# Edge sorting in two parts, with a fixed share of the gathers done during the second part

## The reference

```python
# x [6250,256], src,dst,edge_weight [100000]
x = x + gnn(layernorm(x), W, src, dst, edge_weight)
x = x + moe(layernorm(x))

def gnn(x, W, edge_row, edge_col, edge_val):      # edge_row=src, edge_col=dst
    h = einsum('nd,od->no', x, W)
    msgs = edge_val[:, None] * h[edge_col]
    return segment_sum(msgs, edge_row, num_segments=6250)

def moe(x):
    topk_vals, topk_idx = top_k(x @ gate_w + gate_b, 2)
    h = relu(einsum('bsh,ehf->bsef', x, w1) + b1)
    sel = take_along_axis(einsum('bsef,efh->bseh', h, w2) + b2, topk_idx)
    y = x + sum(softmax(topk_vals) * sel)
    return layernorm(y) * gamma + beta
```

## Time and profile before

| | |
|---|---|
| median of 3 runs | 2410.16 us (2407.57 to 2418.26) |
| profiled execution, first to last instruction (span) | 2018.8 us |
| median less span | 391.4 us |
| busy: PE, PEld | 1467.5 (73%), 1163.1 (58%) |
| busy: DVE, ACT, POOL | 965.3 (48%), 638.6 (32%), 1155.4 (57%) |
| mean granted TensorE clock | 0.850 |
| sort: to the first gather of the sums | 0 to 381.3 us |
| sums: first to last gather | 381.3 to 1436.1 us |

### The profile page before, as it was taken

One profiled execution on the slowest core, in us unless ns is written; L12 is line 12 of the kernel. 1 busy time (PEld: TensorE's weight loads), 2 busy tenths in 40 slices (PEclk: granted clock), 3 DMA queues, 4 the chain that ended last, 5 costly groups with the idle time before them and its releaser, 6 DMA issues. The chain is left out here.

```text
span 2018.8 us, 34171 instructions
## 1 busy us (share of the span) xinstructions
PE 1467.5 (73%) x7822; PEld 1163.1 (58%) x7823; DVE 965.3 (48%) x2285; ACT 638.6 (32%) x1737; POOL 1155.4 (57%) x1167
## 2 busy tenths in 40 slices
PE   7006889477777776777767777767369999999964
PEld 4005888344454554545545554545249999988853
DVE  8999999433323233233253233343653333333348
ACT  4624999000011110110110100101444544444465
POOL 1001444577777777777777777777615554544534
PEclk9558999677788888787778788878789999999987
DMA  5102000233333333333333333333652222243366
GB/s 178 37 19 75 7 6 6 67 104 104 104 104 104 103 104 104 104 104 104 104 99 103 103 103 104 104 104 104 146 183 70 70 90 86 91 147 125 107 197 219
DMA packets 107317, 201.66 MB, mean 100 GB/s; under 512 B 19988, under 2 KB 68747, under 8 KB 107144
## 3 DMA queue, kind: packets, MB, share of 16 engines
q0 software_dynamic: 52672, 139.93, 23.9%
q1 hardware_dynamic: 39720, 42.83, 6.4%
q10 hardware_dynamic: 14880, 18.35, 2.8%
HBM read 165.17 MB, written 35.86 MB: 100 GB/s over the span
## 5 line engine op out<-in xcount | busy, mean ns | idle before, releaser
L858 POOL DMA_INDIRECT hbuf<-xn_rows,ix x832 | 801.0, 963 | 267.9 <-issue 233.2
L950 PE MATMUL bank<-hbuf,picks 128*128 x2032 | 649.4, 461 | 288.3 <-SPq L846 287.7
L950 PEld LDWEIGHTS bank<-hbuf,picks 128*128 128x128 f32 x2032 | 417.4, 223 | 502.2 <-issue 448.6
L887 DVE TENSOR_SCALAR picks<-iota_two,marks 128x256 f32<-128x256 f32 x832 | 330.6, 441 | 677.2 <-PE bank L950 660.2
L1022 ACT ACTIVATE agg<-bank 128x256 f32<-128x256 f32 x49 | 18.8, 383 | 850.3 <-PE bank L950 850.3
L406 POOL DMA_INDIRECT edge_groups<-work,dest_i x56 | 80.7, 1441 | 279.9 <-DVE work L637 267.1
L766 PE MATMUL bank<-work 128*128 128x192 bf16 x1568 | 146.7, 251 | 115.2 <-DVE work L630 115.2
L1568 PEld LDWEIGHTS bank<-rowsT,w_sb 128*128 128x128 f32 x1744 | 212.3, 193 | 28.8 <-issue 24.1
L1568 PE MATMUL bank<-rowsT,w_sb 128*128 128x128 f32 x1744 | 215.7, 277 | 17.7 <-issue 17.7
L1504 POOL DMA_INDIRECT expert_out<-y_sb,to_i x112 | 111.1, 992 | 185.9 <-DVE y_sb L1613 183.0
L1578 PE MATMUL bank<-w_sb,hT 128*128 128x256 f32 x872 | 206.9, 380 | 0.0
(11 more groups left out here) (261 smaller groups left out, 1411.6 us busy)
## 6 DMA issues: line engine op xcount, KB each, us to landing
w_sb<-in_L_ffn_w_dram ACTq DMA_DIRECT2D x28, 512.0 KB, 4.9
hbuf<-xn_rows,ix POOLq DMA_INDIRECT x832, 2.8
xn_rows<-xn SPq DMA_DIRECT2D x11, 896.0 KB, 4.1
x<-in_x_dram SPq DMA_DIRECT2D x6, 896.0 KB, 11.4
ya<-expert_out SPq DMA_DIRECT2D x5, 896.0 KB, 5.6
yb<-expert_out SPq DMA_DIRECT2D x5, 896.0 KB, 7.7
xn_rows<-x SPq DMA_DIRECT2D x3, 896.0 KB, 4.1
w_sb<-in_L_ffn_w_dram SPq DMA_DIRECT2D x4, 512.0 KB, 6.0
```

The source lines that it names most:

```text
L858: pool.indirect_dma_start(hbuf[:, 1 + j, k, :], None, xn_dram, bass.IndirectOffsetOnAxis(ap=ix[:, 2 * j + k:2 * j + k + 1], axis=0)).then_ ...
L887: s = v.tensor_scalar(picks[:, j % 2, k, :], iota_two[:], marks[:, 0, 2 * j + k:2 * j + k + 1], marks[:, 1, 2 * j + k:2 * j + k + 1], ALU. ...
L950: m = nc.tensor.matmul(bk[q][:, 0:D], picks[:, j, k, q * P:(q + 1) * P], hbuf[:, ds(place + j, 1), k, :].rearrange("p s d -> p (s d)"), st ...
```

## The change

The sort of the first 4 columns is now finished before the second part is placed. Its groups are listed apart: of each window the first 32 groups (`FG`: 4 tiles, `FT`) go into a list of their own, 196 tiles in all (`FTILES`). What the first part has beyond 32, and all of the second part, go into the list of the sums as before. While DVE places and sorts the other 10 columns, POOL gathers the 196 tiles one by one into 16 buffers, DVE makes a pick for each (128 wide, in 6 buffers), TensorE sums four of them into one bank per window, ScalarE copies the sum to `fsum`, and SP stores it to DRAM (`first_sums`). At the start of the sums SP loads these rows back, and a window's bank begins with them (a matmul with `ident`) instead of with zeros. The gate work of TensorE leaves the batches and stands between the two parts. The tables of the sums are all made at the end of the sort. The 196 tiles are spread over the second part by numbers written into the code: 60 until the batches begin, 168 by the last batch, the other 28 behind it.

```diff
     PARTS = [(0, 4), (4, 14)]
+    FIRST = PARTS[0][1]
+    FT = 4
+    FG = FT * TILE_GROUPS
+    FTILES = NW * FT
...
+        PLACE_TILES, SORT_TILES = 60, 168
+        def tiles_by_batch(n):
+            done = n + 1 - FIRST_BATCHES
+            return PLACE_TILES + done * (SORT_TILES - PLACE_TILES) // (BATCHES - FIRST_BATCHES)
+        def tiles_by_gate(w):
+            return (w + 1) * PLACE_TILES // NW
...
             def _(pool):
-                for c in range(NC):
-                    scatter(c)
+                def gather(s):
+                    if s == 0:
+                        pool.wait_ge(tables_ready, 1)
...
+                    if s >= RH:
+                        pool.wait_ge(first_used, s - RH + 1)
+                    pool.indirect_dma_start(fbuf[:, s % RH, :], None, xn_dram,
+                                            bass.IndirectOffsetOnAxis(ap=fdst_i[:, s:s + 1], axis=0)).then_inc(xn_gathered[s % RH], 16)
+                for c in range(FIRST):
+                    for k in range(KG):
+                        scatter(c, k)
...
+                for c in range(FIRST, NC):
+                    taken_by = min((c + 1) * NBATCH + 2, BATCHES - 1)
+                    for k in range(KG):
+                        while gathered < tiles_by_batch(taken_by) + RH - 6 + k:
+                            gather(gathered)
+                            gathered += 1
+                        scatter(c, k)
+                for s in range(gathered, FTILES):
+                    gather(s)
...
             def _(dve):
-                mark(1)
+                for t0 in range(0, CT, MC):
+                    if t0 >= 2 * MC:
+                        dve.wait_ge(seen_counted, t0 // MC - 1)
+                    mark(1, t0, seen[t0 // MC % 2]).then_inc(hot_ready, 1)
...
                 starts(0)
-                place(0)
...
-                starts(1)
-                place(1)
-                dve.sem_inc(placed, 1)
...
-                destinations()
+                factors(0)
+                starts(1)
+                listing()
+                first_destinations()
+                factors(1)
+                place(0, first_factors)
...
+                for n in range(FIRST_BATCHES):
                     hots(n)
                     fill(n)
...
+                take(FIRST - 1)
+                for t0 in range(0, CT, MC):
+                    mark(1, t0, hot[1][:, t0:t0 + MC, :, :])
+                for b in range(FBLK):
+                    dve.wait_ge(recs_turned, b + 1)
+                    table(b, turned_0(b), min(P, FTILES - b * P), fdst_i, frow_f, fwgt_f, tables_ready)
+                picks_to(2)
+                turns()
+                def picks_in_place(t):
+                    picks_to(2 + t * (PLACE_TILES - 2) // (CT + 8))
+                place(1, picks_in_place)
+                rest_destinations()
+                picks_to(PLACE_TILES)
+                for n in range(FIRST_BATCHES, BATCHES):
+                    hots(n)
+                    fill(n)
+                    picks_to(tiles_by_batch(n) + 2)
...
+                def picks_to(tiles):
+                    while picked < min(tiles, FTILES):
+                        s = picked
+                        if s >= RK:
+                            dve.wait_ge(first_used, s - RK + 1)
...
             def _(pe):
+                def sum_to(tiles):
+                    while used < min(tiles, FTILES):
+                        w, t = divmod(used, FT)
+                        if t == 0 and w >= 2:
+                            pe.wait_ge(first_summed, w - 1)
+                        pe.wait_ge(first_picked, used + 1)
+                        pe.wait_ge(xn_gathered[used % RH], 16 * (used // RH + 1))
+                        nc.tensor.matmul(bk[w % 2][:, 0:D], fpicks[:, used % RK, :], fbuf[:, used % RH, :],
+                                         start=t == 0, stop=t == FT - 1).then_inc(first_used, 1)
...
-                    nc.tensor.matmul(bk[q][:, 0:D], nil[:, 0:P], nil[:], start=True, stop=False, skip_group_check=True)
+                    nc.tensor.matmul(bk[q][:, 0:D], ident[:], first_sums[:, ds(w, 1), :].rearrange("p w d -> p (w d)"), start=True, stop=False, skip_group_check=True)
```

More of the change, by code:

```diff
@@ L10, in __init__ @@
     def __init__(self, engine, done):
[L11 to L20, removed]
+        self.engine, self.done, self.n = engine, done, 0
     def __call__(self, instruction):
@@ L24, in __call__ @@
         self.n += 1
-        self.engine.wait_ge(self.done, self.turn * self.per + (self.base + self.n))
+        self.engine.wait_ge(self.done, self.n)
 def await_turn(engine, sem, turn, per, value):
@@ L219, in gnn_moe_kernel @@
         by_field = work[:, fields_at:fields_at + TBLK * 2 * P].rearrange("p (b f e) -> p b f e", b=TBLK, f=2)
[L221 to L230, removed]
+        rest_from = place_at
+        rec_rows = again(TBLK, TILE_GROUPS, 2 * RG).rearrange("p b g (f s) -> p b g f s", f=2)
+        place_at = rest_from
+        passed_1 = again(KG, N1, NW + 1)
+        delta_1 = again(N1, NW + 1)
+        step_1 = again(N1, NW + 1)
+        gw_1, gpos_1 = again(NW, N1), work[:, 0:NW * N1].rearrange("p (w c) -> p w c", w=NW)
+        place_at = past_hot
+        gw_0, gpos_0 = again(NW, FIRST), again(NW, FIRST)
+        passed_0 = again(KG, FIRST, NW + 1)
+        delta_0 = again(2, FIRST, NW + 1)
+        step_0 = again(2, FIRST, NW + 1)
+        listed_f = again(2, KG, FIRST)
+        listed_w, listed_p = again(KG, FIRST), again(KG, FIRST)
+        listed_i = again(KG, FIRST).bitcast(i32)
         FAR, ROWS_FROM = 2, 12
@@ L438, in normalize @@
                     s.then_inc(xn_ready, 1)
+                act.wait_ge(iota_two_set, 2)
+                act.sem_inc(act_steps, 1)
+                for h, rows in enumerate((iota_f, iota_next)):
+                    act.activation(iota_rows[:, h * P:(h + 1) * P, :], rows[:, :, None].to_broadcast([P, P, 2]), ACT.Copy).then_inc(rows_set, 1)
                 for k, (numbers, unit) in enumerate(((low_i, 1.0), (code, 256.0), (dst_e, 65536.0))):
@@ L535, in _, with place @@
                 added = numbers = 0
-                def place(a):
+                def place(a, between):
                     nonlocal added, numbers
@@ new lines, in listing @@
+                def listing():
+                    link(v.tensor_copy(gw_0, groups[:, 0:FIRST, :].rearrange("p c w -> p w c")))
+                    v.tensor_reduce(gsum[:], groups[:].rearrange("p c w -> p w c"), AX.X, ALU.add)
+                    link(v.tensor_reduce(first_n[:], gw_0, AX.X, ALU.add))
+                    link(v.tensor_scalar(taken[:], first_n[:], float(FG), None, ALU.min))
+                    link(v.tensor_tensor(wsum[:], gsum[:], taken[:], ALU.subtract))
+                    link(v.tensor_scalar(wsum[:], wsum[:], float(LEAST), None, ALU.max))
@@ L596, in destinations, with turns @@
+                def turns():
+                    tile_shift = TILE_GROUPS.bit_length() - 1
                     v.memset(quad_i[:, 0:1], 1)
@@ L795, in gnn_moe_kernel @@
         aggT = [sb(f"aggT{q}", [P, NB, P], fp32) for q in range(2)]
-        gathered = [sem(f"gathered{j}") for j in range(PR)]
         ix_set = sem("ix_set")
@@ L889, in body @@
                         s.then_inc(pick_ready, 1)
-                        if isinstance(i, int) and j == 1:
-                            for b in range(1, TBLK):
-                                table(v, dve, link, b, code_2)
                         if j == 2 and not isinstance(i, int):
```

454 lines of the change are left out of this document (304 added, 150 removed).

## The result

The changed kernel takes 2378.49 us (median of 4 runs, 2374.57 to 2384.60) against 2413.76 us for the kernel before (4 runs, 2407.57 to 2418.26): 0.985 of it, with a 95% interval of 0.9817 to 0.9883. That is 35 us less, where 62 were forecast.

The account below looks back on a forecast made before the run. POOL's gathers, 1.268 us each, were taken to bound the sums stage. Sort +184, sums -248.5 and load +2 gave -62 us, so 2410 - 62 = 2348 us, range 2290 to 2405.

Parts of the forecast that it names:

- What bounds the kernel now: Whole kernel: sums go at POOL's pace, 1.268 us a gather; 391.4 us between span and median carried over unchanged.
- What is removed: Sums: 196 tiles fewer at 1.268 us, 248.5 us off; load of the stored sums adds 2 us.
- rival E: Sums: they don't shrink in full, since TensorE falls behind at low clock; about 2410 us, chance 0.08.
- (a) to (d): Sort, first part to second marking: first batch at 103 us, marking over at 183.5, first new gather at 191.
- POOL under DVE: Sort: each scatter waits for the DVE instruction it meets, then takes 0.93 us; gathers taken to behave as scatters.
- rival B: Sort: gathers aren't blocked by DVE; sort +117, time 2281 us; chance 0.12 for under 2310.
- C: Sort: all transfers blocked, 1.77 us each; sort +237, time 2401 us; chance 0.12 for 2385 to 2410.
- (e): Placement of the second part: its sums and 52 picks wait for 46 gathered tiles, 68 us, ending at 259 us.
- (f): Sort, after the placement's sums: tree, tail, picks, waits and remaining destinations; batches begin at 296 us.
- (g): 40 batches of the second part: POOL the bound, 5.4 us a batch, 215 us, ending at 511.
- Rival D: Batches: TensorE's clock falls to 1.2 GHz, 7.2 us a batch; 2421 us if it stays there; chance 0.10.
- (h), (i): End of the sort: 13 gathers and 4 scatters, last scatter at 533 us; tables, last tiles, store; sums' first gather 565.

Follow-up runs that it names:

- e1: The kernel before, unchanged, profiled and timed again: 2436.80 us (10 runs).
- e2: The changed kernel, unchanged, profiled and timed again: 2399.97 us, 0.9819 of before.
- e6: The changed kernel with quotas 4 and 8 instead of 60 and 168, so nearly all first-part gathers come behind the last scatter: 1.0109 of before.
- e8: The changed kernel with quotas 40 and 140 instead of 60 and 168: 0.9827 of before.
- e3: The kernel before, with the matmuls of the sums taking 64 of the 256 columns: 2364.30 us, against 2417.59 for before beside it.
- e5: The changed kernel with five added bf16 matmuls behind each pair of tiles in the sums, to keep TensorE busy: 2506.42 us, 1.0369 of before.

## Why the prediction came out as it did

**What bounds the kernel now.** Here is the step that failed: "the median is 391.4 us more. I put the sum on the span and carry the 391.4 over unchanged, since nothing behind the sums changes." The 391.4 us do not lie outside the span: it was 420 us shorter than that of e1. 397 us of these are the longer way from the first to the last gather (1450.5 against 1053.9) and 23 a longer tail (606.4 against 583.7); the sort is the same to 0.4 us. The reading that the sums go at POOL's pace of 1.268 us, with nothing to wait for, falls with it: in e1 POOL waits once per 16 gathers, and a gather takes 1.746 us. Only because the 391.4 us were added back unchanged did the level of the forecast come out. A profile whose span is 16% below every timed run had to be doubted before any sum was built on it.

**What is removed.** 248.5 us were taken, at 1.268 us a gather. Between e1 and e2 it is 1450.5 - 1185.6 = 265: 192 gathers fewer (26 rings to 20) at 1.746 are 335 us less, and the other 640 cost 0.11 us more each, 70 us, since a gap grew from 8.0 to 9.8 us per 16 gathers. That may come from the windows' ends, which now lie closer together (49 on 640 gathers instead of 832); this is argued and was not tried. So rival E was right in kind, that the sums don't shrink in full because TensorE falls behind. The load of the stored sums wasn't seen apart.

**(a) to (d).** They held: first batch 102 (forecast 103), second marking over at 182.7 (183.5), four scatters of 3.3 to 3.7 us beneath it, first new gather 191.16 (191).

**POOL under DVE.** Held, and for gathers too: the one issued at 284.18 ends 0.83 us after DVE's L673 of 7.15 us. The mean of a gather in the sort is 1.232 us, and 0.988 where few lie under the batches (e6). So rival B is out, and so is C: not all of them are held. The Trainium skill's list ("SBUF — State Buffer", section "Who interferes with whom") that says such a DVE instruction didn't slow transfers issued by GpSimd is contradicted by this trace for scatters and for gathers.

**(e), placement.** The first term mis-sized: 259 was forecast for its end, it was 283.5, 24.5 us more. I let POOL set the pace of the chain gather, matmul, pick. In the waits of that stretch DVE waits for TensorE, which runs at a granted clock of 0.70 there and has the gate work too (us in total, times, longest wait):

```profile
DVE dst_e L823 <- PE bank L986: 17.0, 17, 2.4
DVE dst_e L823 <- remote: 15.9, 4, 6.6
```

e8, with 20 tiles fewer there, ends it 17 us earlier. How much of the 24.5 us is the clock, the gate work or slow phases was not tried.

**(f)** took 33 us where 37 were forecast.

**(g), batches.** 215 us forecast, 237 measured, and not by an even 5.4 us. The median period is 4.4, near DVE's own 4.1; seven of 40 are over 8 us and hold 81 us. The waits from the first batch to the last:

```profile
DVE dst_e L823 <- remote: 36.2, 7, 14.4
...
DVE dst_e L823 <- PE bank L986: 21.6, 12, 4.0
...
POOL fbuf L479 <- PE bank L986: 13.5, 10, 10.8
```

So the 22 us over the forecast lie mostly in a few long batches, like the one above of 15.9 us, in which TensorE's slow phase holds DVE through the pick's wait for the tile six before; POOL was not the bound throughout. Rival D named a lower clock for this; the granted clock from 300 to 500 us is 0.88, so D did not happen, though its place, the chain gather, matmul, pick, was the right one.

**(h), (i).** From the last batch to the first gather of the sums 54.7 us, 54 forecast, with the parts shifted: 12.6 to the last scatter, then 42.1.

**Together.** Sort +227 to +237 instead of +184 (43.5 us too low, all of it in (e) and (g) less a few us), gathers -265 instead of -246.5, tail -3: -31 between the spans of e1 and e2. The sort was put 43 to 53 us too low and the gathers' saving 18.5 us too low, so the errors partly cancelled: that 35 us came out of 62 and not less is in part luck. Rival B's sum has a slip as well: with 76 gathers out, 92 and 36 scatters are 128 transfers, not 133, 6 us less, which decides nothing. With the short lead in both kernels the change is worth 2248.1 - 2170.6 = 77.5 us of span: sort +229.9, gathers -309.0, tail +1.6.

## What to carry to other kernels

Compare a profile's span with the timed runs before reading it; where the two differ by far more than in other runs (here 391 us instead of 1.8), it may show another regime, and prices per item must come from an execution that is like the timed ones. Where a fast producer may run far ahead of an engine that stalls now and then, a shorter lead can be faster, and the handshake that really holds it back must be looked up (here 16 row numbers at a time, not 16 buffers): one constant gave 7% (before) and 9% (changed kernel) here, the change itself 1.5 to 1.8%. Work moved beneath another stage is worth its price in the stage it left, minus what it costs in the stage it enters: 1.7 against 1.06 us a tile here, and the price in the new stage was set in good part by the waits that tie DVE to TensorE, not by either engine's busy time alone.

## What was not expected of the hardware

TensorE has slow phases, of 5 to 15 us at the full lead and mostly under 10 at a short one, in which it and its queue advance in steps of 0.7 us, while the granted clock in the records stays at 0.5 or 1.0. They come in the sums stage of all 13 profiles taken since the one of before (without a matmul for over 5 us TensorE is there 33 times in 1160 us in the changed kernel, 52 times in 1451 in e1, 3 times in 1054 in the profile of before), in the sort once gathers and fp32 sums run in it, and not in the experts' stage, where TensorE is busy for over 80% of 600 us. The Trainium skill ("TensorE: Matmul & The Clock Gate", section "Seeing it yourself") warns that the clock records are unreliable and tells of a peak-current limit, which one or two busy cores never trip; here one core is busy, so by the page this is something else; no run here shows what. What sets a slow phase off stays open: fewer columns (e3, with the weight loads unchanged) and a busier TensorE (e5) did not end them, the lead of POOL changed their length, and one execution of the kernel before had none.
